# Three loser lists in place of two, paired list loads, and chain steps by twos in an edge convolution

## What is computed

```
h = relu(layernorm(x))                       # over the 128 features, eps 1e-5
feat = concat([h[dst], h[src] - h[dst]])     # per edge
msg = feat @ W.T + b
out = segment_max(msg, dst, num_segments=6250)
x + where(isfinite(out), out, 0)
```

## Time and profile before

| | us |
|---|---|
| median of 3 runs | 853.31 (853.27 to 854.31) |
| profiled execution | 851.91 |
| its span, first to last instruction | 850.3 |
| DVE busy | 774.5 (91%) |
| GpSimd (POOL) busy | 604.4 (71%) |
| TensorE (PE) matmuls | 544.2 (64%) |
| ScalarE busy | 422.4 (50%) |

### The profile page before, as it was taken

One profiled execution on the slowest core, in us unless ns is written; L12 is line 12 of the kernel. 1 busy time (PEld: TensorE's weight loads), 2 busy tenths in 40 slices (PEclk: granted clock), 3 DMA queues, 4 the chain that ended last, 5 costly groups with the idle time before them and its releaser, 6 DMA issues.

```text
span 850.3 us, 7998 instructions
## 1 busy us (share of the span) xinstructions
PE 544.2 (64%) x2442; PEld 263.4 (31%) x2442; DVE 774.5 (91%) x1251; ACT 422.4 (50%) x279; POOL 604.4 (71%) x630
## 2 busy tenths in 40 slices
PE   1574899000002877767666686888888888888870
PEld 1553467000001322223222232333333333333340
DVE  6989999989997998899898999999999998888896
ACT  3786313250274365665657669555555557560000
POOL 1577277777777767677777777777777677777773
PEclk9999799555555998899888998999999999999995
DMA  8961013323456655545655455556665655642336
GB/s 256 222 156 24 9 36 96 93 74 93 137 146 188 200 167 141 176 141 177 175 138 171 142 179 140 177 183 187 182 191 174 195 190 169 216 139 77 101 102 203
DMA packets 114693, 126.74 MB, mean 149 GB/s; under 512 B 19542, under 2 KB 96836, under 8 KB 114379
## 3 DMA queue, kind: packets, MB, share of 16 engines
q1 hardware_dynamic: 95090, 86.33, 33.4%
q0 software_dynamic: 19376, 38.94, 17.6%
q10 hardware_dynamic: 184, 0.96, 0.3%
HBM read 86.43 MB, written 40.57 MB: 149 GB/s over the span
## 4 chain that ended last, share of the span: by engine, by line
DVE 35%; PE 18%; issue 14%; DVEq 0%
DVE acc L1326 20%; PE ps L862 18%; DVE maxima L1270 10%; DVE hT L1279 2%; DVE hT L1383 1%; DVE hT L1293 1%; DVE hT L1284 1%; DVEq L1325 0%; DVE hT L1385 0%; DVE M L1298 0%; PE ps L850 0%; DVEq L1266 0%; DVEq L887 0%; DVEq L1283 0%; DVE spare L1304 0%
## 5 line engine op out<-in xcount | busy, mean ns | idle before, releaser
L739 POOL DMA_INDIRECT rows<-near_table,idx x503 | 503.5, 1001 | 181.0 <-issue 135.8
L1326 DVE TENSOR_TENSOR acc<-ps,acc 128x1924 f32<-128x1924 f32 x196 | 343.7, 1779 | 33.8 <-PE ps L862 33.5
L862 PE MATMUL ps<-ohs,near 128*128 128x481 fp8e3 x1404 | 320.1, 382 | 84.7 <-DVE acc L1326 76.4
L601 ACT ACTIVATE ohs<-ohs,spike 128x6272 fp8e3<-128x6272 uint8 x36 | 197.8, 5513 | 71.9 <-DMA ohs<-winners 71.9
L862 PEld LDWEIGHTS ps<-ohs,near 128*128 128x128 bf16 x1404 | 134.6, 101 | 270.1 <-DVE acc L1326 94.9
L1270 DVE SCALAR_TENSOR_TENSOR maxima<-maxima,fresh,rows 128x128 f32<-128x128 f32 x503 | 176.8, 352 | 13.6
L596 ACT ACTIVATE hT<-k,off 128x1600 bf16<-128x1600 int16 (+6 forms) x49 | 65.8, 1391 | 146.8 <-DVE hT L1284 146.8
L862 PE MATMUL ps<-sorts_mem,near 128*128 128x481 fp8e3 x507 | 114.3, 379 | 29.0 <-DVE acc L1326 26.9
L601 ACT ACTIVATE sorts_mem<-sorts_mem,spike 128x6272 fp8e3<-128x6272 uint8 x13 | 71.7, 5515 | 28.7 <-DMA sorts_mem<-winners 28.7
L850 PE MATMUL ps<-flags,ones 128*128 128x11 f32 x2 | 0.6, 363 | 121.7 <-DVE spare L1304 121.7
L862 PEld LDWEIGHTS ps<-sorts_mem,near 128*128 128x128 bf16 x507 | 48.6, 100 | 94.5 <-DVE acc L1326 31.7
(11 more groups left out here) (183 smaller groups left out, 436.1 us busy)
## 6 DMA issues: line engine op xcount, KB each, us to landing
running_max<-maxima SPq DMA_DIRECT2D x63, 512.0 KB, 3.6
ohs<-winners SPq DMA_DIRECT2D x36, 784.0 KB, 6.3
sorts_mem<-winners SPq DMA_DIRECT2D x13, 784.0 KB, 6.1
rows<-near_table,idx POOLq DMA_INDIRECT x503
acc<-in_x SPq DMA_DIRECT2D x6, 512.0 KB, 7.2
near_table<-acc SPq DMA_DIRECT2D x12, 256.0 KB
base<-in_x SPq DMA_DIRECT2D x1, 2744.0 KB
out_x<-hT SPq DMA_DIRECT2D x12, 224.0 KB
```

What stands on the lines that cost most here:

```text
L601: nc.scalar.activation(oh[t % OHS], oh_bytes[t % OHS], ACT.Abs_reciprocal_sqrt, bias=spike[:, 0:1], scale=float(SPIKE), saturate=False).th ...
L739: nc.gpsimd.indirect_dma_start(rows[:, n % (SLOTS * GATHERS), :], None, near_table[:, :], bass.IndirectOffsetOnAxis(idx[:, n:n + 1], 0)).t ...
L862: last = nc.tensor.matmul(bank(4 * (n % 2) + c - UNITS[r][0])[:, 0:CHUNK], near[:, t, part, :], oh[t % OHS][:, at:at + CHUNK], start=part ...
L1326: V.tensor_tensor(into, found[:, 0:z - a, 0:CHUNK], into, ALU.max).then_inc(max_done, 1)
```

## The change

- Three lists of 7, 14 and 28 columns, which give 64, 128 and 312 steps; 40 and 64 losers per partition are carried on. `first_words` becomes `counted_words(h)` for the first two, `second_words` becomes `last_words`. The lists of 14 and 28 columns are both pieces of the plan.
- One indirect load brings 128 sources, 64 ahead of a node's first edge and 64 behind it, so that it holds a node and, turned round, the node before it. 24 or 25 such loads replace 49 of 64; `src_pad` gets 64 zeros in front. The masks of odd and even columns are made apart (`from_end`).
- The window of `dst` is gathered in two parts, 1,027 and 1,169 edges, and each group of 8 targets searches only a stretch of it (735 to 1,091 elements). Three further flags check that the stretch was right, and send the data the slow way if not.
- `MOST_STEPS` goes from 4 to 2, and the planner counts a first step 0.26 and a following one 0.38, and other piece costs.
- On SP's queue the fourth chunk of x waits for the near window, the base load for the first list's loads, and the check's loads move behind the stores of near_table.

```diff
-PARTS = ((0, 15, 136), (15, 49, 368))
+LOOK_FROM, LOOK_FROM_STEP = -76, 236
+LOOK_TO, LOOK_TO_STEP = 735, 292
+NEAR_SPAN = LOOK_TO + LOOK_TO_STEP
+PARTS = ((0, 7, 64), (7, 21, 128), (21, 49, 312))
+LEFT = (0, 40, 64, 0)
-LANDING, MARGIN, MOST_STEPS = 4.6, 1.5, 4
+LANDING, MARGIN, MOST_STEPS = 4.6, 1.5, 2
+STEP, NEXT_STEP = 0.26, 0.38
...
-            now += 0.355
+            now += NEXT_STEP if here else STEP
...
                 if c == 3:
-                    sp.wait_ge(begin_ready, 1)
+                    sp.wait_ge(win_in[0], 16)
...
-            sp.wait_ge(win_in, 16)
-            sp.wait_ge(chk_pad_set, 1)
-            sp.dma_start(chk_i[0:chk_p, 0:chk_w], dst.rearrange("(p t) -> p t", t=chk_w)).then_inc(chk_in, 16)
+            sp.wait_ge(list_in[0], 16 * loads_of(0))
             sp.wait_ge(base_pad_set, 1)
...
-            nc.gpsimd.indirect_dma_start(win_i, None, dst[:, None],
-                                         bass.IndirectOffsetOnAxis(begin_i[:, 0:1], 0)).then_inc(win_in, 16)
-            pool.wait_ge(pad_in, 32)
+            nc.gpsimd.indirect_dma_start(win_i[:, 0:NEAR_SPAN], None, dst[:, None],
+                                         bass.IndirectOffsetOnAxis(begin_i[:, 0:1], 0)).then_inc(win_in[0], 16)
+            pool.wait_ge(far_ready, 1)
+            nc.gpsimd.indirect_dma_start(win_i[:, NEAR_SPAN:WIN], None, dst[:, None],
+                                         bass.IndirectOffsetOnAxis(far_i[:, 0:1], 0)).then_inc(win_in[1], 16)
+            pool.wait_ge(pad_in, 48)
             for h, (a, z, _) in enumerate(PARTS):
                 pool.wait_ge(starts_ready, h + 1)
-                for j in range(a, z):
-                    nc.gpsimd.indirect_dma_start(L[:, j, :], None, src_pad[:, None],
+                for j in range(a + a % 2, z, 2):
+                    nc.gpsimd.indirect_dma_start(L_pairs[:, j // 2, :], None, src_pad[:, None],
                                                  bass.IndirectOffsetOnAxis(start_i[:, j:j + 1], 0)).then_inc(list_in[h], 16)
...
-                for c in range(a, z, 8):
-                    then(V.max_index(pos[:, c:c + 8], tgt[:, c:c + 8], win))
+                for k in range(a // 8, z // 8):
+                    look = win[:, max(0, LOOK_FROM + k * LOOK_FROM_STEP):min(LOOK_TO + k * LOOK_TO_STEP, WIN)]
+                    then(V.max_index(pos[:, 8 * k:8 * k + 8], tgt[:, 8 * k:8 * k + 8], look))
...
-            find(0, 16)
+            find(0, 8)
             begins(0)
             statistics(1)
-            find(16, 32)
+            dve.wait_ge(win_in[1], 16)
+            then(V.tensor_scalar(win[:, NEAR_SPAN:WIN], win_i[:, NEAR_SPAN:WIN], fill[:, 0:1], None, ALU.max))
+            settled()
+            find(8, 24)
+            begins(1)
+            find(24, 56)
+            begins(2)
             scales(1)
...
-                for u, v in in_parts(0, KS, MOST_AT_ONCE // (q - a)):
-                    then(V.tensor_tensor(S1[:, u:v, a:q], iota_f[:, u:v, None].to_broadcast([P, v - u, q - a]),
-                                         deg[:, None, a:q].to_broadcast([P, v - u, q - a]), ALU.is_ge))
+                for j, place in ((a + a % 2, iota_f), (a + 1 - a % 2, from_end)):
+                    n = len(range(j, q, 2))
+                    for u, v in in_parts(0, KS, MOST_AT_ONCE // n):
+                        then(V.tensor_tensor(S1[:, u:v, j:q:2], place[:, u:v, None].to_broadcast([P, v - u, n]),
+                                             deg[:, None, j:q:2].to_broadcast([P, v - u, n]), ALU.is_ge))
```

More of the change, by code:

```diff
@@ L55, with steps_before, places, kept @@
 J_BIAS = 2
-def stages(h):
-    a, z, _ = PARTS[h]
-    return ((z - a) * KS + LEFT * h - 1).bit_length()
-FLAG_PIECES, WORD_PIECES = 6, 5
+def steps_before(h):
+    return sum(c for _, _, c in PARTS[:h])
+def places(h):
+    a, z, _ = PARTS[h]
+    return (z - a) * KS + LEFT[h]
+def kept(h):
+    return PARTS[h][2] + LEFT[h + 1]
+def stages(h):
+    return (places(h) - 1).bit_length()
+def in_parts(at, end, most=MOST_AT_ONCE):
+    parts = -(-(end - at) // most)
+    marks = [at + (end - at) * i // parts // 2 * 2 for i in range(parts)] + [end]
+    return list(zip(marks, marks[1:]))
+def stride_of_spots(h, i):
+    d = 1 << i
+    return 2 * d if 2 * d >= 2 * kept(h) or i == stages(h) - 1 else 0
 EARLY_TREES = 6
@@ L98, in schedule @@
 def schedule():
[L103 to L113, removed]
@@ L114, in schedule @@
-    pieces += [("list", 2.2, 1.4), ("verdict", 0.2, 1.3)]
-    pieces += [("disorder", 0.8, 1.3)]
+    pieces, trees = [], 0
+    for h in range(1, LAST + 1):
+        columns = PARTS[h][1] - PARTS[h][0]
+        share = columns / 34
+        pieces += [("lists", h, 0.6 + 10.8 * share, 2.0)]
+        if h == 1:
+            pieces += [("check", h, 1.1, 1.6), ("check", h, 1.9, 1.6), ("check", h, 1.9, 1.6)]
+        pieces += [("sort", h, 0.3 + 1.14 * share, 1.5)] * 21
+        if h == LAST:
+            pieces += [("tiles", h, 2.3, 1.7)]
+        pieces += [("flags", h, 0.4 + cost * share, 1.7) for cost in (2.0, 2.5, 2.4, 2.4, 1.2)]
+        if h == LAST:
+            pieces += [("words", h, cost, 1.7) for _ in in_parts(0, places(h)) for cost in (1.3,)]
+            pieces += [("words", h, cost, 1.7) for cost in (2.6, 1.2, 2.6)]
+        else:
+            pieces += [("words", h, cost, 1.7) for cost in (2.1, 1.5, 2.0, 1.8)]
+        for i in range(stages(h)):
+            end = places(h) - (1 << i)
+            if stride_of_spots(h, i):
+                pieces += [("move", h, 0.6, 1.5), ("move", h, 1.0, 1.5)]
+            else:
+                pieces += [("move", h, 0.1 + 0.00062 * end, 1.5)]
+                pieces += [("move", h, 0.1 + 0.00128 * (v - u), 1.5) for u, v in in_parts(0, end)]
+            if h == LAST and TREES_FROM <= i < TREES_FROM + EARLY_TREES:
+                pieces += [(name, h, cost, 1.6) for name, cost in tree_pieces(trees)]
+                trees += 1
+        pieces += [("list", h, 2.2, 1.4)]
@@ L116, in schedule @@
+    pieces += [("verdict", LAST, 0.2, 1.3), ("disorder", LAST, 0.8, 1.3)]
     for t in range(49):
         for r in range(4):
[L118 removed]
+            pieces += [("round", LAST, (2.1, 1.6, 1.6, 1.6)[r], 1.26)]
         if trees < 25:
[L120 removed]
+            pieces += [(name, LAST, cost, 1.3) for name, cost in tree_pieces(trees)]
             trees += 1
[L122 removed]
+    total = steps_before(LAST + 1)
@@ L123, in schedule @@
+    first_of = {steps_before(h): h for h in range(1, LAST + 1)}
     finals = {FINALS_FROM + g * FINALS_EVERY: GROUP for g in range(CUTS[0][0] // GROUP)}
-    now, issue, n, landed, done, listed, steps = 0.0, 0.0, 0, [], [], None, []
-    for name, cost, gather in pieces:
+    now, issue, n, landed, done, listed, steps = 0.0, 0.0, 0, [], [], {}, []
+    for name, h, cost, gather in pieces:
         now += cost
         if name == "list":
-            listed = now
+            listed[h] = now
         here = []
@@ L150, in schedule @@
         steps.append(here)
-    return [name for name, _, _ in pieces], steps, list(range(n, total)), first, total
+    return [(name, h) for name, h, _, _ in pieces], steps, list(range(n, total)), total
 def edgeconv(nc, x, src, dst, W, b, out):
```

255 lines of the change are left out of this document (151 added, 104 removed).

## The result

The changed kernel takes 840.66 us (median of four, 840.01 to 841.41) where the kernel before takes 853.81 on the same chip: a ratio of 0.9852, with a 95% interval of 0.984 to 0.9864. The forecast was 841.0. The profiled execution took 840.78 us.

A forecast was written before the change was run, and what follows sets the result against it. VectorE sets the pace, TensorE adds to it. The first round starts 10.8 us later; rounds shorten by 18.9 (steps) and 4.0 (waits), ending 12.1 earlier: median 853.31 to 841.2, likeliest 841, range 831 to 850.

The forecast's parts named there:

- The search: Ahead of the first list: shorter searches and waits that go save 12.7 us, bounds 8 and 14; list begins at 36.3.
- The first list: List of 7 columns: 34.4 us in all, ready at 70.7 where it was at 106.9.
- Three lists and 64 pairs: From first list to first round: lists of 14 and 28 columns 173.4 us, 64 pairs 42.2; first round at 286.3.
- the sum was to end 2 to 4 us earlier: Ahead of the rounds: by the skill page's fixed latency, 97 further list instructions cost 15 us, not the sort line's 19.
- Steps: Chain steps: pairs at 0.66 us for fours at 1.42; 180 pairs between the rounds take 118.8 for 137.7, 18.9 less.
- Waits for TensorE: In the rounds: VectorE's waits for matmuls, 30.0 us before, shrink by 4, bounds 0 and 10.
- the clock: Rival, chance 0.10: longer TensorE idle gaps behind nine other tree tiles lower its clock; 859 us if all nine fall.
- 6-step tiles: In the rounds: tiles with six steps become bound by TensorE, 8.8 us plus some 0.3 gap, taking back 1 to 2.
- The rounds: The 196 dense rounds: 545.8 us less 18.9 for steps and 4.0 for waits, 522.9, ending at 809.2.
- The gathers are a condition that is met.: GpSimd's gathers don't bound: it waits 15.8 us for chain steps, and no VectorE wait for a gather is seen.
- the pairs' 12.2: Whole chain: two steps in a row instead of four free 12.2 us of VectorE in all.
- eaten ahead of the rounds: Rival, chance 0.12: lists and search cost 8 to 12 us more than counted; 849 to 853, first round 295 or later.

The follow-up runs named there:

- experiment 3: The changed kernel with six of its seven searches over the whole window of 2,196 elements again: 846.57 us, ratio 0.9919 to the kernel before.
- experiment 4: The changed kernel with up to three chain steps behind a piece instead of two: 840.88 us, ratio 0.984 to the kernel before.
- experiment 7: The changed kernel with each tree's pieces spread over the fourth round of its tile and the next tile's first three: 826.37 us, ratio 0.9666.
- experiment 12: The changed kernel, trees unmoved, with matmuls that nobody reads filling TensorE's idle time behind each tree: 825.59 us, ratio 0.9688 to the kernel before.
- experiment 6: The changed kernel with its gathers held some 34 us, to about where the kernel before had its first gather: 851.25 us, ratio 0.9974.
- experiment 2: The kernel before with two chain steps in a row at most instead of four, nothing else: ratio 0.9959, about 850.4 us; median of all twelve 852.15.
- experiment 11: The kernel before with its trees spread over the fourth round and the next tile's first three: 849.26 us, ratio 0.9945.

## Why the prediction came out right

- **The search.** Forecast -12.7, measured -11.94. Six full searches put back cost 7.9 us ahead of the first list, forecast 7.7, and 5.9 in the end (experiment 3).
- **The first list.** Forecast 34.4, ready at 70.7; measured 35.48, ready at 72.50. The last near_table store was issued at 56.1, forecast 60 to 64.
- **Three lists and 64 pairs.** Forecast 215.6, measured 287.38 - 72.50 = 214.88. Inside it is a wait that I had not named, 2.48 us for a store of maxima, so the pieces themselves were 3 us cheaper than forecast. The Trainium skill, "VectorE: DVE Perf Modes", on the TRN2 errata, gives an instruction from SBUF a fixed latency of about 150 cycles, by which the sum was to end 2 to 4 us earlier; the 3 us agree, though no run separates the fixed part of a piece from the part for its words.
- **Steps.** Most pairs in the rounds cost 0.64 or 0.65, and on average, with the dearer ones, the forecast 0.66. The groups of four of before cost 1.44 on average and not 1.42. The steps take 119.4 us in place of 139.3, so 19.9 are saved where the text has 18.9. The rule behind it, a first step at 0.28 and a further one at 0.38, survived the threes of experiment 4.
- **Waits for TensorE: the term that was mis-sized.** Forecast 4 off with bounds of 0 and 10; measured 0.9 *more*, just outside. By the waits view of the two stretches, without the wait ahead of the first round, the tiles after the trees fell from 17.5 to 15.3 us, and the first 20, with the trees, rose from 12.5 to 15.5. The sum reckoned only with the first kind; what lay behind the second was the clock, whose falls it had under the rivals alone (experiments 7 and 12 take 15.4 and 14.4 us of these waits away). In the tiles behind the trees, 6-step tiles were to be "bound by TensorE" at about 9.1 us, but five of the seven there repeat after 9.42, as 550.60 - 541.18 below, as long as an 8-step one, and only two after 9.05. So most of the steps left out of them gave nothing back.

```profile
541.18 2.16 DVE L1422 TENSOR_TENSOR acc<-ps,acc 128x1924 f32<-128x1924 f32 x1 [0.62 <-PE ps L928]
...
550.60 2.16 DVE L1422 TENSOR_TENSOR acc<-ps,acc 128x1924 f32<-128x1924 f32 x1 [0.59 <-PE ps L928]
```

- **The rounds**, forecast 522.9, took 810.44 - 287.38 = 523.06. The agreement is better than its parts, and in part luck: of the 22.8 us, 19.9 came from the steps. Another 3.2 came from rounds and trees (372.9 us for 376.0), which the sum had left as they were: a round of 1,443 columns takes 1.57 us where a step follows it and 1.61 to 1.66 where another round does, and there are now more groups of steps. A wait of 0.5 went, and the waits for TensorE took 0.8 to 0.9 back. So two errors of nearly 5 us each cancelled: TensorE's waits, forecast 4 shorter, grew by 0.9, and steps, rounds and trees gave that much more than the text has.
- **"The gathers are a condition that is met."** True of the changed kernel, and too weak. They are met *because* the first list is earlier: hold them back and 851 comes out (experiment 6), take the pairs without the list and 850 to 852 (experiment 2), spread the trees without it and 849 (experiment 11). The sum gave the three lists a cost of 16.8 us and the search a gain of 12.7, and credited them with nothing else; that the pairs' 12.2 could only be cashed with them stood nowhere. The sum was right since it was made for the whole change. Made for either part alone, the same terms would have missed by 5 us (the lists and the search) and by 11 (the pairs).
- **The rivals.** The gain was not eaten ahead of the rounds (287.38, not 295). The clock fell ten times in the rounds, as before, and did not make the kernel slower; but it was the largest loss in the rounds all the time, some 15 us (experiments 7 and 12), and I had treated it as a danger and not as a price already paid. GpSimd's waits for the chain grew by 13.4 us, not 20 or more.

## What to carry to other kernels

An engine off the critical path may sit just under it: GpSimd's gathers nearly filled their time, so the pairs were worth 2 to 4 us with the late first list and 22.6 with the early one, and spreading the trees 5 and 14. Before crediting a saving, add up the next engine's own work from its first possible start to the end. And where one engine works in long blocks between short rounds, look at what its partner's clock does after them: spreading the block, with no instruction more or less, was worth as much as the whole change.

## What the runs showed of the hardware

The length of an idle time doesn't decide alone whether TensorE's granted clock falls. In the changed kernel it fell to 0.50, the level of 1.2 GHz, behind 2.11 us, and not behind 3.10:

```profile
399.73 5.53 PE L928 MATMUL ps<-sorts_mem,near 128*128 128x481 fp8e3 x18 [2.11 <-DVE acc L1422]
```

```profile
337.75 2.02 PE L928 MATMUL ps<-ohs,near 128*128 128x481 fp8e3 x9 [3.10 <-DVE acc L1422]
```

The Trainium skill, "TensorE: Matmul & The Clock Gate", under why it matters, warns of idle gaps over about 3 us; the first of these rows lies under it and fell, the second lies over it and didn't. Matmuls whose result is never read kept the clock up as well as useful ones did (experiment 12). And a fall need not cost time: the five left in experiment 7 stood where VectorE had little to catch up, and its waits for TensorE in those tiles came to 0.1 us.
